# MLP stage: second layer ahead of the transposes, and two low-half subtractions moved from VectorE to GpSimd

## The chip, the cores and the metric

The kernel runs on one core of a Trainium2 chip. The metric is the device time of one execution in microseconds (us). The engines of the core run their own instruction queues and wait for each other through semaphores: TensorE (PE, with its weight loads PEld), VectorE (DVE), ScalarE (ACT), GpSimd (POOL), and SyncE (SP), which here only issues transfers.

## What is computed

The input x has 4 sequences of 1024 tokens of 256 float32 values. A mixture-of-experts feed-forward, an attention block with its own MLP, and the feed-forward again are added to x in turn:

```python
def _ln(x, s, b):
    mu = jnp.mean(x, axis=-1, keepdims=True)
    var = jnp.mean(jnp.square(x - mu), axis=-1, keepdims=True)
    return (x - mu) * jax.lax.rsqrt(var + EPS) * s + b
...
    att = jnp.einsum('bhqk,bhkd->bhqd', p, v).transpose(0, 2, 1, 3).reshape(Bq, Sq, AHD)
    h = att @ Wo + bo + x
    y = _ln(h, lnm_s, lnm_b)
    m = jax.nn.gelu(y @ W1 + b1) @ W2 + b2
    return m + h
...
    x = x + 0.5 * _L0_ffn_ref(_layernorm(x, axis=-1), ...)
    x = x + _L0_attn_ref(_layernorm(x, axis=-1), ...)
    x = x + 0.5 * _L0_ffn_ref(_layernorm(x, axis=-1), ...)
    return x
```

The change lies in the second line of this: att @ Wo with its residual (h), the layer norm of h, and the two-layer MLP (256 to 512 to 256, tanh form of gelu) with its residual.

## The kernel before

The program runs four stages one behind the other: the first feed-forward (names f_), attention (a_), the MLP stage (m_, function mlp_phase), the second feed-forward (g_). Attention leaves its output in HBM as att, transposed; the first feed-forward has left x1 and its layer norm z there. The MLP stage writes x2.

Every float32 matmul is made of three in the type fp32r: each operand is split into a high half (the value rounded to that type, made by ScalarE) and a low half (the value minus the high half), and high x high, high x low and low x high are summed. So each operand costs one ScalarE pass and one subtraction.

The MLP stage goes over the 4096 tokens in 8 blocks of 512 (NB = 8, BT = 512, NT = 4 tiles of 128 rows). For block i:

- SP loads att in two halves (att_in, 1 MB each, L1361), z (zin, 0.5 MB, L1393) and x1 (xin, 0.5 MB, L1405), and stores res (L1401).
- att_hi (ScalarE, L1418) and att_lo (VectorE, L1510) split each half of att, 128 x 2048 elements, into att_s. att_in has one buffer for each half; att_s, zin and xin have two.
- proj (TensorE, L1593): 96 matmuls, in two halves of 48.
- h = proj + zin (VectorE, L1545); statistics (L1548, L1553); rs = (var + eps) ^ -0.5 (GpSimd, L1495, L1497); hn = (h - mean) * rs, four operations of 128 x 256 (VectorE, L1564).
- 8 transposes of hn into PSUM (hT_ps, TensorE, L1623), split by hT_hi (ScalarE, L1440) and hT_lo (VectorE, L1575).
- hid (TensorE, L1649): first layer, 24 matmuls; gelu (ScalarE, L1424); hid_hi (ScalarE, L1432) and hid_lo (VectorE, L1515), four of each.
- acc (TensorE, L1634): second layer, 48 matmuls.
- GpSimd adds bias rows to zin and xin, four operations each (L1478), and adds h to xin (x_h, L1500). res = acc + xin (VectorE, L1584).

The order of the work is written out by hand. Each engine has a function body(i, par), called for i = 0, for pairs of steps in a loop, and for the last ones; in body i the blocks are staggered: the projection is that of block i+1, acc and res are those of block i-1, att_hi and att_lo those of block i+2. An engine issues in program order and stops at each wait. TensorE's body before is: first half of proj(i+1), transposes(i), acc(i-1), second half of proj(i+1), hid(i). SP's body issues z(i+1) behind h(i); then the att loads of block i+3, each behind the att_lo of its half of block i+2; then the store of res(i-1); and last the load of x1(i+1), behind the bias adds of block i, with no way round what stands ahead.

The helper stand_alone(eng, turns) puts an increment of a semaphore that nobody waits for ahead of an instruction.

Of the kernel before, what the change touches and what calls it, by code (L numbers as in the profile page):

```python
# [20 lines left out]
F32 = mybir.dt.float32  # L21
F32R = mybir.dt.float32r
U32 = mybir.dt.uint32
ALU = mybir.AluOpType
# [3 lines left out]
P = 128  # L28
# [7 lines left out]
DC = D // P  # L36
BT = 512
NT = BT // P
# [7 lines left out]
def stand_alone(eng, turns):  # L46


    eng.sem_inc(turns, 1)
# [1238 lines left out]
def mlp_phase(nc, turns, tag, w, att, z, x1, x2):  # L1288
# [9 lines left out]
    with ExitStack() as ctx:  # L1298
# [39 lines left out]
        def over_steps(eng, body):  # L1338

            body(0, 0)  # L1340
            with eng.Fori(0, (NB - 4) // 2) as it:
                body(it * 2 + 1, 1)
                body(it * 2 + 2, 0)
            for i in range(NB - 3, NB + 1):
                body(i, i % 2)

        def has(i, ahead=0):

            return not isinstance(i, int) or 0 <= i + ahead < NB
# [120 lines left out]
        @block.gpsimd  # L1470
        def _(pool):
            pool.memset(mhalf[:], -0.5).then_inc(s["mhalf"], 1)
            pool.wait_ge(s["mhalf"], 1)
            pool.wait_ge(s["w_in"], 16 * NW)

            def add_rows(x, row):
                for t in range(NT):
                    o = pool.tensor_tensor(x[:, t], x[:, t], row[:], ALU.add)  # L1478
                return o

            def z_bias(i, par):
                pool.wait_ge(s["z_in"], i * 16 + 16)
                add_rows(zin[:, par], bo).then_inc(s["zb"], 1)

            def x_bias(i, par):
                pool.wait_ge(s["x_in"], i * 16 + 16)
                add_rows(xin[:, par], b2).then_inc(s["x_b"], 1)
            z_bias(0, 0)

            def body(i, par):  # L1490
                if has(i):
                    x_bias(i, par)
                    pool.wait_ge(s["stats"], i + 1)
                    stand_alone(pool, turns)
                    pool.tensor_scalar(rs[:], mv[:, :, 1], EPS, None, ALU.add).then_inc(s["veps"], 1)  # L1495
                    pool.wait_ge(s["veps"], i + 1)
                    pool.tensor_tensor(rs[:], rs[:], mhalf[:], ALU.pow).then_inc(s["rstd"], 1)  # L1497

                    pool.wait_ge(s["x_b"], i + 1)
                    pool.tensor_tensor(xin[:, par], xin[:, par], h[:], ALU.add).then_inc(s["x_h"], 1)  # L1500
                if has(i, 1):
                    z_bias(i + 1, 1 - par)
            over_steps(pool, body)

        @block.vector
        def _(dve):
# [6 lines left out]
            def hid_lo(i, hc):  # L1513
                dve.wait_ge(s["hid_hi"], i * HC + hc + 1)
                dve.tensor_tensor(hid_s[:, hc, 1], act_out[:, hc], hid_s[:, hc, 0].bitcast(F32),  # L1515
                                  ALU.subtract).then_inc(s["hid_lo"], 1)
# [21 lines left out]
            def body(i, par):  # L1538
                if has(i):
                    dve.wait_ge(s["proj"], i + 1)  # L1540
                    dve.wait_ge(s["zb"], i + 1)
                    if has(i, -1):

                        dve.wait_ge(s["x_h"], i)
                    dve.tensor_tensor(h[:], proj[:], zin[:, par], ALU.add).then_inc(s["h"], 1)  # L1545
                    dve.wait_ge(s["h"], i + 1)
                    for t in range(NT):
                        o = dve.bn_stats(st6[:, t], h[:, t])  # L1548
                    o.then_inc(s["bn"], 1)
                    dve.wait_ge(s["bn"], i + 1)  # L1550
                    stand_alone(dve, turns)
                    for t in range(NT):
                        o = dve.bn_aggr(mv[:, t], st6[:, t])  # L1553
                    o.then_inc(s["stats"], 1)
                if has(i, -1):
                    hid_lo(i - 1, 0)
                    hid_lo(i - 1, 1)
                if has(i):
                    dve.wait_ge(s["rstd"], i + 1)
                    if has(i, -1):  # L1560

                        dve.wait_ge(s["hT_ps"], i * DC)
                    for t in range(NT):
                        o = dve.tensor_scalar(hn[:, t], h[:, t], mv[:, t, 0:1], rs[:, t:t + 1],  # L1564
                                              ALU.subtract, ALU.mult)
                    o.then_inc(s["hn"], 1)
                if has(i, -1):
                    hid_lo(i - 1, 2)
                    hid_lo(i - 1, 3)
                if has(i, 2):  # L1570
                    att_lo(i + 2, par, 0)
                if has(i):
                    for c in range(DC):
                        dve.wait_ge(s["hT_hi"], i * DC + c + 1)
                        dve.tensor_tensor(hT[:, c, 1], hT_ps[:, c], hT[:, c, 0].bitcast(F32),  # L1575
                                          ALU.subtract).then_inc(s["hT_lo"], 1)
                if has(i, 2):
                    att_lo(i + 2, par, 1)
                if has(i, -1):
                    dve.wait_ge(s["acc"], i)  # L1580
                    dve.wait_ge(s["x_h"], i)

                    dve.wait_ge(s["res_out"], i * 16)
                    dve.tensor_tensor(res[:], acc[:], xin[:, 1 - par], ALU.add).then_inc(s["res"], 1)  # L1584
# [3 lines left out]
        def _(pe):  # L1588
# [21 lines left out]
            def body(i, par):  # L1610
                if has(i, 1):
# [1 line left out]

                    pe.wait_ge(s["h"], i + 1)
                    project(i + 1, 1 - par, (0, 1))
                if has(i):
                    pe.wait_ge(s["hn"], i + 1)
                    if has(i, -1):

                        pe.wait_ge(s["hT_lo"], i * DC)  # L1620
                    for c in range(DC):
                        for t in range(NT):
                            o = pe.transpose(hT_ps[:, c, t * P:(t + 1) * P], hn[:, t, c * P:(c + 1) * P], ident[:])  # L1623
                        o.then_inc(s["hT_ps"], 1)
                if has(i, -1):

                    pe.wait_ge(s["hid_lo"], i * HC)
                    if not has(i):

                        pe.wait_ge(s["res"], i - 1)  # L1630
                    for t in range(NT):
                        for hc in range(HC):
                            for a, b in PARTS:
                                o = pe.matmul(acc[:, t], hid_s[:, hc, a, t * P:(t + 1) * P], w2[:, b, hc],  # L1634
                                              start=(t % 2 == 0 and hc == 0 and (a, b) == (0, 0)),
                                              stop=(hc == HC - 1 and (a, b) == PARTS[-1]), skip_group_check=True)
                    o.then_inc(s["acc"], 1)
                if has(i, 1):
                    project(i + 1, 1 - par, (2, 3)).then_inc(s["proj"], 1)
                if has(i):  # L1640
# [81 lines left out]
```

## Time and profile before

| What | Value |
|---|---|
| time of the profiled execution | 2578.13 us |
| its span | 2575.9 us |
| median of 3 runs (lowest, highest) | 2577.75 us (2575.99, 2578.18) |
| MLP stage, first proj matmul to last acc matmul | 2064.8 to 2284.8 us |
| PE busy in the span | 2443.0 us (95%) |
| DVE | 1910.3 us (74%) |
| ACT | 1674.7 us (65%) |
| POOL | 1499.4 us (58%) |

The busy shares say little about the MLP stage, which is 8.5% of the span and in which DVE (142 of 220 us) and POOL (87 of 220) have other shares than in the whole. The timeline of single engines within the stage shows more: a row is a run of equal instructions, with its start, its length, and in brackets how long the engine had been idle before it and which instruction ended that. An idle bracket on TensorE is time lost in this stage if TensorE has work ready behind it.

### The profile page before, as it was taken

Reading aid. Unit: us, or ns where it says so; the run is one execution under the profiler, and the core shown is the slowest. Engines: PE = TensorE matmul, PEld = TensorE weight load, DVE = VectorE, ACT = ScalarE, POOL = GpSimd, SP = SyncE. Lnnn points to the kernel's source line nnn. Section 1 sums busy time; section 2 is a strip of 40 time slices with the busy share of each in tenths; the row PEclk is TensorE's granted clock in tenths of the full one; section 3 lists DMA queues with packets and bytes.
Section 4 is the critical chain, followed back from the end, with each engine's and each line's share of the span. In section 5 each row is a group of like instructions: output and inputs, shape, how many; then the busy total and the mean of one; then the engine's idle time right before and its main releaser. Section 6 shows DMA issues by size and latency. Waiting matters only on the chain. (4 is left out here: it accounts for less than half of the span.)

```text
span 2575.9 us, 46634 instructions
## 1 busy us (share of the span) xinstructions
PE 2443.0 (95%) x14544; PEld 2110.3 (82%) x14544; DVE 1910.3 (74%) x3637; ACT 1674.7 (65%) x2887; POOL 1499.4 (58%) x1519
## 2 busy tenths in 40 slices
PE   6999779999999999999999999999999689959999
PEld 5888768888888888888888888888888488948888
DVE  6777457878878788787887878878778566646665
ACT  3555357878778787787877877778778534233333
POOL 2333167777777777778767777677776244322221
PEclk9999799999999999999999999999999899979999
DMA  4222432213212132122321222212221253321111
GB/s 161 84 96 90 165 116 65 91 49 99 92 43 86 58 95 93 41 82 67 88 90 41 82 81 74 90 41 91 77 70 50 102 174 123 99 88 34 49 49 41
DMA packets 133706, 212.85 MB, mean 83 GB/s; under 512 B 12564, under 2 KB 95816, under 8 KB 125000
## 3 DMA queue, kind: packets, MB, share of 16 engines
q1 hardware_dynamic: 133576, 211.48, 25.5%
q8 instruction: 37, 0.61, 0.1%
q14 instruction: 93, 0.76, 0.1%
HBM read 112.88 MB, written 48.25 MB: 63 GB/s over the span
## 5 line engine op out<-in xcount | busy, mean ns | idle before, releaser
L1168 DVE TENSOR_REDUCE a_nmax<-a_sc 128x1 f32<-128x1024 f32 x512 | 626.6, 1224 | 263.3 <-PE a_sc L1238 253.9
L1099 POOL TENSOR_SCALAR a_pr<-a_pr,a_rden 128x1024 f32<-128x1024 f32 x512 | 575.9, 1126 | 287.7 <-DVE a_rden L1173 226.8
L1029 ACT ACTIVATE a_pT<-a_tr 128x512 fp32r<-128x512 f32 x1024 | 559.6, 596 | 242.1 <-PE a_tr L1250 233.0
L1179 DVE TENSOR_TENSOR a_pT<-a_tr,a_pT 128x512 fp32r<-128x512 f32 x1024 | 650.2, 677 | 18.3 <-ACT a_pT L1029 18.3
L1271 PE MATMUL a_ov<-a_pT,a_v_s 128*128 128x512 f32 x2048 | 604.9, 417 | 1.3 <-DVE a_half L1159 1.3
L1035 ACT ACTIVATE a_pr<-a_sc,a_nmax 128x1024 f32<-128x1024 f32 x512 | 573.7, 1120 | 18.8 <-DVE a_nmax L1168 15.5
L1238 PE MATMUL a_sc<-a_k_s,a_q_s 128*128 128x512 f32 x2048 | 559.7, 395 | 0.4 <-POOL a_v_b L1065 0.4
L1250 PEld LDWEIGHTS a_tr<-a_ident,a_pr 128*128 128x128 f32 x4096 | 475.0, 140 | 96.3 <-DVE a_pT L1179 16.7
L1250 PE MATMUL a_tr<-a_ident,a_pr 128*128 128x128 f32 x4096 | 537.3, 273 | 12.3 <-POOL a_pr L1099 6.2
L1238 PEld LDWEIGHTS a_sc<-a_k_s,a_q_s 128*128 128x128 f32 x2048 | 380.8, 188 | 86.3 <-issue 0.5
L1271 PEld LDWEIGHTS a_ov<-a_pT,a_v_s 128*128 128x128 f32 x2048 | 346.7, 189 | 54.2 <-issue 3.4
L1199 PE MATMUL a_pj<-a_z_s,a_wqk_s 128*128 128x512 f32 x756 | 197.2, 396 | 16.0 <-DMA a_z_s<-zT 15.1
L1199 PEld LDWEIGHTS a_pj<-a_z_s,a_wqk_s 128*128 128x128 f32 x756 | 142.7, 189 | 50.2 <-issue 16.8
L338 ACT ACTIVATE g_act_out<-g_hid,g_b 128x512 f32<-128x512 f32 x72 | 49.6, 689 | 154.9 <-PE g_hid L677 154.9
L1001 ACT ACTIVATE a_staged<-a_pj,a_bqk_s 128x512 f32<-128x512 f32 x126 | 87.1, 691 | 77.1 <-PE a_pj L1199 77.1
L338 ACT ACTIVATE f_act_out<-f_hid,f_b 128x512 f32<-128x512 f32 x72 | 49.3, 684 | 113.8 <-PE f_hid L677 113.8
L709 PEld LDWEIGHTS f_acc<-f_w2p,f_hp 128*128 128x128 f32 x864 | 113.2, 191 | 11.1 <-DVE f_hp L524 5.8
L709 PE MATMUL f_acc<-f_w2p,f_hp 128*128 128x256 f32 x864 | 116.6, 285 | 3.9 <-DVE f_hp L524 3.4
L677 PE MATMUL g_hid<-g_xT,g_w1p 128*128 128x512 f32 x432 | 118.0, 410 | 1.2 <-DVE g_w1p L569 1.2
L677 PE MATMUL f_hid<-f_xT,f_w1p 128*128 128x512 f32 x432 | 117.6, 409 | 1.2 <-DVE f_w1p L569 1.2
L709 PEld LDWEIGHTS g_acc<-g_w2p,g_hp 128*128 128x128 f32 x864 | 111.9, 189 | 7.7 <-DVE g_hp L524 2.1
L709 PE MATMUL g_acc<-g_w2p,g_hp 128*128 128x256 f32 x864 | 115.0, 282 | 0.7 <-DVE g_hp L524 0.5
(220 smaller groups left out, 3219.4 us busy)
## 6 DMA issues: line engine op xcount, KB each, us to landing
a_z_s<-zT SPq DMA_DIRECT2D x32, 1024.0 KB, 7.0
a_k_s<-a_k_s SPq DMA_DIRECT2D x64, 512.0 KB, 5.7
a_wqk_s<-w_split SPq DMA_DIRECT2D x64, 256.0 KB, 3.0
a_v_s<-a_v_b SPq DMA_DIRECT2D x16, 1024.0 KB, 4.6
att<-a_ao SPq DMA_DIRECT2D x32, 512.0 KB, 2.9
m_att_in<-att SPq DMA_DIRECT2D x16, 1024.0 KB, 5.4
a_wv_s<-w_split SPq DMA_DIRECT2D x17, 512.0 KB, 3.8
zT<-f_zT SPq DMA_DIRECT2D x8, 1024.0 KB, 3.9
```

The lines of the kernel that those rows point to most:

```text
L338: act.activation(act_out[:, e % 3], hid[:, (par + e) % 2], ACT.Gelu, bias=b1[:, weights_of(e):weights_of(e) + 1]).then_inc(s["gelu"], 1)
L677: o = pe.matmul(hid[:, (par + e) % 2], w1p[:, a, (c * NE + x) * HID:(c * NE + x + 1) * HID], xT[:, par, c, b], start=(n == 0), stop=(n == 5))
L709: o = pe.matmul(acc[:, t], hp[:, e % 3, a, t * P:(t + 1) * P], w2p[:, b, x * D:(x + 1) * D], start=False, stop=(e == NE - 1 and (a, b) == ...
L1029: act.activation(pT[:, (u // 4) % 2, 0, 4 * part:4 * part + 4, (u % 4) * P:(u % 4 + 1) * P], tr[:, part].rearrange("p (t q) -> p t q", t=4 ...
L1035: act.activation(pr[:, k % NP], sc[:, k % 2], ACT.Exp, bias=nmax[:, k % NP:k % NP + 1], accum_out=den[:, k % NP:k % NP + 1]).then_inc(s["e ...
L1099: pool.tensor_scalar(pr[:, k % NP], pr[:, k % NP], rden[:, k % NP:k % NP + 1], 1.0, ALU.mult, ALU.mult).then_inc(s["normed"], 1)
L1168: dve.tensor_reduce(nmax[:, k % NP:k % NP + 1], sc[:, k % 2], AX.X, ALU.max, negate=True).then_inc(s["negmax"], 1)
L1179: dve.tensor_tensor(to[:, 1], tr[:, part].rearrange("p (t q) -> p t q", t=4), to[:, 0].bitcast(F32), ALU.subtract).then_inc(s["tr_lo"], 1)
L1199: o = pe.matmul(bank[:], wqk_s[:, "QK".index(kind), c, a], z_s[:, c * 2 + b, part], start=(i == 0), stop=(i == 5))
L1238: o = pe.matmul(sc[:, k % 2, kb * BT:(kb + 1) * BT], q_s[:, slot, head, tile * P:(tile + 1) * P], k_s[:, slot, head, a, kb * BT:(kb + 1) * ...
L1250: o = pe.transpose(tr[:, part, j * P:(j + 1) * P], pr[:, (k - LAG) % NP, (4 * part + j) * P:(4 * part + j + 1) * P], ident[:])
L1271: o = pe.matmul(ov[:], v_s[:, vslot, kt, 2 * vhead:2 * vhead + 2] .rearrange("p k f -> p (k f)"), pT[:, blk % 2, a, kt], start=(kt == 0 an ...
```

## The change

In TensorE's body acc(i-1) goes ahead of transposes(i). In VectorE's body the four hid_lo stand together ahead of hn, and the att_lo of blocks 2 to 7 are gone; those of blocks 0 and 1, ahead of the loop, stay on VectorE. GpSimd's body gets them: half 0 behind the residual sum x_h, half 1 behind the bias adds of zin. They wait for att_hi of the same half and for the count of att_lo so far.

```diff
@@ -1487,6 +1487,15 @@
                 add_rows(xin[:, par], b2).then_inc(s["x_b"], 1)
             z_bias(0, 0)
 
+            def att_lo(i, par, half):
+                pool.wait_ge(s["att_hi"], i * 2 + half + 1)
+
+                pool.wait_ge(s["att_lo"], i * 2 + half)
+                stand_alone(pool, turns)
+                g = slice(half * HP, (half + 1) * HP)
+                pool.tensor_tensor(att_s[:, par, 1, g], att_in[:, half], att_s[:, par, 0, g].bitcast(F32),
+                                   ALU.subtract).then_inc(s["att_lo"], 1)
+
             def body(i, par):
                 if has(i):
                     x_bias(i, par)
@@ -1498,8 +1507,12 @@
 
                     pool.wait_ge(s["x_b"], i + 1)
                     pool.tensor_tensor(xin[:, par], xin[:, par], h[:], ALU.add).then_inc(s["x_h"], 1)
+                if has(i, 2):
+                    att_lo(i + 2, par, 0)
                 if has(i, 1):
                     z_bias(i + 1, 1 - par)
+                if has(i, 2):
+                    att_lo(i + 2, par, 1)
             over_steps(pool, body)
 
         @block.vector
@@ -1553,8 +1566,8 @@
                         o = dve.bn_aggr(mv[:, t], st6[:, t])
                     o.then_inc(s["stats"], 1)
                 if has(i, -1):
-                    hid_lo(i - 1, 0)
-                    hid_lo(i - 1, 1)
+                    for hc in range(HC):
+                        hid_lo(i - 1, hc)
                 if has(i):
                     dve.wait_ge(s["rstd"], i + 1)
                     if has(i, -1):
@@ -1564,18 +1577,11 @@
                         o = dve.tensor_scalar(hn[:, t], h[:, t], mv[:, t, 0:1], rs[:, t:t + 1],
                                               ALU.subtract, ALU.mult)
                     o.then_inc(s["hn"], 1)
-                if has(i, -1):
-                    hid_lo(i - 1, 2)
-                    hid_lo(i - 1, 3)
-                if has(i, 2):
-                    att_lo(i + 2, par, 0)
                 if has(i):
                     for c in range(DC):
                         dve.wait_ge(s["hT_hi"], i * DC + c + 1)
                         dve.tensor_tensor(hT[:, c, 1], hT_ps[:, c], hT[:, c, 0].bitcast(F32),
                                           ALU.subtract).then_inc(s["hT_lo"], 1)
-                if has(i, 2):
-                    att_lo(i + 2, par, 1)
                 if has(i, -1):
                     dve.wait_ge(s["acc"], i)
                     dve.wait_ge(s["x_h"], i)
@@ -1613,15 +1619,6 @@
 
                     pe.wait_ge(s["h"], i + 1)
                     project(i + 1, 1 - par, (0, 1))
-                if has(i):
-                    pe.wait_ge(s["hn"], i + 1)
-                    if has(i, -1):
-
-                        pe.wait_ge(s["hT_lo"], i * DC)
-                    for c in range(DC):
-                        for t in range(NT):
-                            o = pe.transpose(hT_ps[:, c, t * P:(t + 1) * P], hn[:, t, c * P:(c + 1) * P], ident[:])
-                        o.then_inc(s["hT_ps"], 1)
                 if has(i, -1):
 
                     pe.wait_ge(s["hid_lo"], i * HC)
@@ -1635,6 +1632,15 @@
                                               start=(t % 2 == 0 and hc == 0 and (a, b) == (0, 0)),
                                               stop=(hc == HC - 1 and (a, b) == PARTS[-1]), skip_group_check=True)
                     o.then_inc(s["acc"], 1)
+                if has(i):
+                    pe.wait_ge(s["hn"], i + 1)
+                    if has(i, -1):
+
+                        pe.wait_ge(s["hT_lo"], i * DC)
+                    for c in range(DC):
+                        for t in range(NT):
+                            o = pe.transpose(hT_ps[:, c, t * P:(t + 1) * P], hn[:, t, c * P:(c + 1) * P], ident[:])
+                        o.then_inc(s["hT_ps"], 1)
                 if has(i, 1):
                     project(i + 1, 1 - par, (2, 3)).then_inc(s["proj"], 1)
                 if has(i):
```

TensorE, one body of the loop. m_proj are the projection halves, m_hT_ps the transposes, m_acc the second layer, m_hid the first. Before:

```order
L1593 MATMUL m_proj<-m_wo,m_att_s 128x256 x48
L1623 MATMUL m_hT_ps<-m_ident,m_hn 128x128 x8
L1627 REGISTER_ALU
L1634 MATMUL m_acc<-m_w,m_hid_s 128x256 x48
L1593 MATMUL m_proj<-m_wo,m_att_s 128x256 x48
L1645 REGISTER_ALU
L1649 MATMUL m_hid<-m_hT,m_w 128x512 x12
```

and after:

```order
L1599 MATMUL m_proj<-m_wo,m_att_s 128x256 x48
L1624 REGISTER_ALU
L1631 MATMUL m_acc<-m_w,m_hid_s 128x256 x48
L1642 MATMUL m_hT_ps<-m_ident,m_hn 128x128 x8
L1599 MATMUL m_proj<-m_wo,m_att_s 128x256 x48
L1651 REGISTER_ALU
L1655 MATMUL m_hid<-m_hT,m_w 128x512 x12
```

The 48 acc matmuls have moved from behind the 8 transposes to ahead of them.

GpSimd, one body of the loop (bias adds of x1, rs, the residual sum into m_xin, bias adds of z). Before:

```order
L1478 TENSOR_TENSOR m_xin<-m_xin,m_b 128x256 x4
L1493 REGISTER_ALU
L1495 TENSOR_SCALAR m_rs<-m_mv 128x4
L1497 TENSOR_TENSOR m_rs<-m_rs,m_mhalf 128x4
L1500 TENSOR_TENSOR m_xin<-m_xin,m_h 128x1024
L1482 ISA
L1478 TENSOR_TENSOR m_zin<-m_zin,m_bo 128x256 x4
```

and after:

```order
L1478 TENSOR_TENSOR m_xin<-m_xin,m_b 128x256 x4
L1504 TENSOR_SCALAR m_rs<-m_mv 128x4
L1506 TENSOR_TENSOR m_rs<-m_rs,m_mhalf 128x4
L1509 TENSOR_TENSOR m_xin<-m_xin,m_h 128x1024
L1491 ISA
L1496 TENSOR_TENSOR m_att_s<-m_att_in,m_att_s 128x2048
L1482 ISA
L1478 TENSOR_TENSOR m_zin<-m_zin,m_bo 128x256 x4
L1491 REGISTER_ALU
L1496 TENSOR_TENSOR m_att_s<-m_att_in,m_att_s 128x2048
```

One subtraction of 128 x 2048 stands directly behind the residual sum, one behind the bias adds of z. ISA and REGISTER_ALU rows are semaphore and register work. SP's and ScalarE's instructions stand in the same order as before; their waits on att_lo are now fulfilled by GpSimd.

## Rows read from the trace of the kernel before

**Rows 1.** Timeline, TensorE in the MLP stage: start us, us, engine, line, operation, out<-in [idle before <-releaser]

```profile
2094.85 5.75 PE L1649 MATMUL m_hid<-m_hT,m_w 128*128 128x512 f32 x24
...
2162.78 1.96 PE L1623 MATMUL m_hT_ps<-m_ident,m_hn 128*128 128x128 f32 x8 [2.76 <-DVE m_hn L1564]
2164.43 7.93 PE L1634 MATMUL m_acc<-m_w,m_hid_s 128*128 128x256 f32 x48
...
2177.90 5.76 PE L1649 MATMUL m_hid<-m_hT,m_w 128*128 128x512 f32 x24
2183.50 5.86 PE L1593 MATMUL m_proj<-m_wo,m_att_s 128*128 128x256 f32 x48
2189.19 1.04 PE L1623 MATMUL m_hT_ps<-m_ident,m_hn 128*128 128x128 f32 x8
2190.26 5.94 PE L1634 MATMUL m_acc<-m_w,m_hid_s 128*128 128x256 f32 x48
...
2201.74 5.76 PE L1649 MATMUL m_hid<-m_hT,m_w 128*128 128x512 f32 x24
...
2251.08 5.75 PE L1649 MATMUL m_hid<-m_hT,m_w 128*128 128x512 f32 x24
...
2268.96 5.76 PE L1649 MATMUL m_hid<-m_hT,m_w 128*128 128x512 f32 x24
2277.34 7.47 PE L1634 MATMUL m_acc<-m_w,m_hid_s 128*128 128x256 f32 x48 [2.62 <-DVE m_hid_s L1515]
```

**Rows 2.** Stretches A:B us: length, busy us of each engine, granted clock, DMA share

```profile
2150.00:2175.00 25.00, 22.24 (x147) 21.12 (x146) 16.82 (x22) 9.63 (x12) 9.82 (x11) 0.86 0.34 112
2175.00:2200.00 25.00, 24.97 (x188) 23.64 (x187) 17.19 (x22) 9.53 (x12) 9.82 (x11) 1.00 0.43 136
```

**Rows 3.** Timeline, GpSimd in the MLP stage

```profile
2082.43 1.04 POOL L1497 TENSOR_TENSOR m_rs<-m_rs,m_mhalf 128x4 f32<-128x4 f32 x1
...
2101.01 2.84 POOL L1478 TENSOR_TENSOR m_xin<-m_xin,m_b 128x256 f32<-128x256 f32 x4 [12.25 <-DMA m_xin<-x]
...
2153.32 3.31 POOL L1478 TENSOR_TENSOR m_xin<-m_xin,m_b 128x256 f32<-128x256 f32 x4 [17.45 <-DMA m_xin<-x]
...
2156.91 1.04 POOL L1497 TENSOR_TENSOR m_rs<-m_rs,m_mhalf 128x4 f32<-128x4 f32 x1
...
2160.26 2.97 POOL L1478 TENSOR_TENSOR m_zin<-m_zin,m_bo 128x256 f32<-128x256 f32 x4
2178.94 2.84 POOL L1478 TENSOR_TENSOR m_xin<-m_xin,m_b 128x256 f32<-128x256 f32 x4 [15.71 <-DMA m_xin<-x]
```

**Rows 4.** Timeline, DMA issues on SP's queue

```profile
2094.74 0.51 SPq L1405 DMA_DIRECT2D m_xin<-x  x1
...
2145.04 1.11 SPq L1405 DMA_DIRECT2D m_xin<-x  x1
...
2174.38 0.46 SPq L1405 DMA_DIRECT2D m_xin<-x  x1
```

**Rows 5.** Timeline, ScalarE: the high half of the attention output

```profile
2165.27 1.90 ACT L1418 ACTIVATE m_att_s<-m_att_in 128x2048 fp32r<-128x2048 f32 x1
...
2190.88 1.92 ACT L1418 ACTIVATE m_att_s<-m_att_in 128x2048 fp32r<-128x2048 f32 x1
```

**Rows 6.** Groups by form, GpSimd and VectorE: out<-in, xcount | busy us, mean ns | idle before

```profile
L1126 POOL TENSOR_TENSOR a_ao<-a_ao,a_half 128x1024 f32<-128x1024 f32 x32 | 76.7, 2395 | 10.6 <-ACT a_ao L1022 10.6
L1065 POOL TENSOR_TENSOR a_v_b<-a_staged,a_v_b 128x256 fp32r<-128x256 f32 x64 | 46.9, 733 | 0.0
...
L1179 DVE TENSOR_TENSOR a_pT<-a_tr,a_pT 128x512 fp32r<-128x512 f32 x1024 | 650.2, 677 | 18.3 <-ACT a_pT L1029 18.3
```

**Rows 7.** Timeline of narrow stretches, GpSimd and VectorE: single hn beside GpSimd

```profile
2130.10 2.79 POOL L1500 TENSOR_TENSOR m_xin<-m_xin,m_h 128x1024 f32<-128x1024 f32 x1
...
2130.54 2.50 DVE L1564 TENSOR_SCALAR m_hn<-m_h,m_mv,m_rs 128x256 f32<-128x256 f32 x1
...
2132.96 0.83 DVE L1564 TENSOR_SCALAR m_hn<-m_h,m_mv,m_rs 128x256 f32<-128x256 f32 x1
```

## Prediction

> **What bounds the kernel now.** I read first the TensorE rows of the MLP stage [rows 1]. The reader is to see three things there. T_i below is the start of the first-layer matmuls of block i-1 (hid, L1649), which is the moment the projection of block i ends: T_1 = 2094.85, T_4 = 2177.90, T_5 = 2201.74, T_7 = 2251.08, T_8 = 2268.96. First, an undisturbed step: from T_4 to T_5 the pieces hid, half a projection, transposes, acc, half a projection follow without a gap, 5.6 + 5.7 + 1.07 + 5.8 + 5.7 = 23.84 us. No step can be shorter than this, and the change removes no TensorE work. Second, the six steps from T_1 to T_7 take 156.23 us, 26.04 each, so 13.2 us in all is stall and what follows a stall. Third, the stall is in one place: the transposes wait 2.76 us for hn at 2162.78, and behind that acc takes 7.93 us where it took 5.94 undisturbed, so a stall costs some 2 us more than its length. Over the 25 us with that stall the granted clock was 0.86 of full speed, in the next 25 it was 1.00 [rows 2]: part of that stretch ran at 1.2 GHz, the lower of the two levels.
>
> Then the GpSimd and queue rows, to see why hn is late [rows 3, 4]. The block of x1 is asked for by SP at 2145.04 and GpSimd's row adds begin at 2153.32, 8.28 us later; the adds take 3.31, the two operations for 1/sqrt end at 2157.95, and only then can hn start. So the stage is set by TensorE in its good steps and by the chain "x load, row adds, rs, hn, transposes" in its bad ones. SP issues that x load after it has waited for the att_lo of both halves and for res. The question for the change is what becomes of that chain.
>
> **TensorE: acc ahead of the transposes.** Nothing is added. The good side: the transposes are now due at T + 5.6 + 5.7 + 5.8 = T + 17.1 where they were due at T + 11.3, so hn has 5.8 us more. The acc matmuls need the four hid_lo at T + 11.3; the last step shows that they are there 8.4 us after T when nothing is in their way (acc at 2277.34 against T_8 = 2268.96) [rows 1], and that is still in time with hid_lo 2 and 3 ahead of hn on VectorE. The other side: whatever hangs on the transposes comes 5.8 us later in the step. That is hT_hi, and behind it on ScalarE att_hi of the second half, which ends 3.61 us after a prompt transpose start (2190.88 + 1.92 against 2189.19) and 4.39 us after a slow one (2165.27 + 1.90 against 2162.78) [rows 1, 5]. The first layer's own wait for hT_lo stays covered by the 5.7 us of the second projection half.
>
> **VectorE: two att_lo fewer.** It loses 2 x 2.3 us a step, none of it on a path that ends last in the trace, because they stand behind hn. Worth nothing by itself. What it has left with an input in PSUM (h, hT_lo, res) isn't held by GpSimd: the a_pT operation, PSUM and SBUF in, takes 677 ns on average over 1024 of them while GpSimd is busy most of the time [rows 6].
>
> **GpSimd: two subtractions more.** The trace has no GpSimd tensor_tensor of 2048 elements. It has 2395 ns for 1024 elements and 733 ns for 256 (this one with the same output type) [rows 6]; the slope is 1662 / 768 = 2.16 ns an element, so 2395 + 1024 x 2.16 = 4.6 us. The bounds are 2 x 2.40 = 4.8 above (the start cost paid twice) and 2048 x 2.16 = 4.4 below (no start cost); I take 4.6. GpSimd's step is then 2.85 + 1.4 + 2.4 + 4.6 + 3.0 + 4.6 = 18.9 us of 23.8: it isn't full, but it is now in two chains. The Trainium skill, page "GPSIMD Engine Reference", section 3.1, gives 4497 ns for a tensor_tensor add of 2048 float32 elements and advises VectorE for such work; by its figure the sum below would be 1 us shorter.
>
> *First chain: hn.* An hn that meets a GpSimd operation is held until that operation ends. The first hn at 2130.54 takes 2.50 us, through the whole of the residual sum x_h that runs from 2130.10 to 2132.89; each hn behind it takes 0.83, one GpSimd row add of 0.75 apart [rows 3, 7]. So the pattern is one hn for each GpSimd operation. With att_lo as GpSimd's next operation behind x_h, the first hn ends with x_h (2.4 + 0.15 after rs), the second with att_lo (4.6 later), the third and fourth one z row add apart each (0.75 + 0.75): hn is complete 8.7 us after rs, where it was 4.6 to 4.7. That no row shows a hold of 4.6 us leaves the second of these open. The Trainium skill, page "SBUF — State Buffer", section "SBUF: two separate sides", says of the port pair shared by VectorE and GpSimd that whoever starts first has it for the whole instruction; by that the hold is 4.6 us as I take it, and if 2.4 us, the longest hold in the rows, were a ceiling, the loop below would be 2.2 us shorter and the sum 11.
>
> *Second chain: SP.* SP waits for att_lo of half 1 (block i+2) before it issues the att load of that half, then the res store, then the x load of block i+1. Those two transfers and the x load now stand behind a GpSimd operation that can't begin before att_hi of half 1. This closes a loop through five engines. From the end e of that att_lo:
> - SP issues att, res, x: two issues ahead of x at 0.5 each (their rows last 0.46 to 0.51) and the start: 1.1 [rows 4].
> - x load to GpSimd's first row add: the rows give 4.56 (2174.38 to 2178.94), 6.27 (2094.74 to 2101.01, an att load issued 0.5 ahead) and 8.28 (2145.04 to 2153.32) [rows 3, 4]. The case is that of 6.27 with a res store of half an att load's size in between too. I take the middle of 6.27 and 8.28, 7.3; ends 4.56 and 8.28.
> - x row adds 2.85, rs 1.4 [rows 3].
> - hn 8.7 (above), its signal 0.1.
> - transposes to the end of att_hi: 3.6 to 4.4, I take 4.0.
> - att_lo on GpSimd: 0.1 + 4.6.
>
> Sum: 1.1 + 7.3 + 2.85 + 1.4 + 8.7 + 0.1 + 4.0 + 0.1 + 4.6 = 30.15 us a step, against 26.04 now and 23.84 for TensorE. TensorE with a slow stretch of 2 to 3 us in each step would need 26 to 27, so it waits and the loop sets the step.
>
> **The sum.** Block 0: rs ends at 2083.47 as before [rows 3]; hn 2092.2, transposes 2092.3, first e = 2092.3 + 4.0 + 0.1 + 4.6 = 2101.0. The loop runs until block 5 (att_lo of block 7 is the last): e of block 4 = 2101.0 + 4 x 30.15 = 2221.6. The transposes of block 5 stand 1.1 + 7.3 + 2.85 + 1.4 + 8.7 + 0.1 = 21.45 later, at 2243.0. Then 1.04 + 5.7 to T_6, and one undisturbed step, because block 6 has no att_lo and no att load on its way: T_7 = 2243.0 + 6.74 + 23.84 = 2273.6, against 2251.08: **+22.5**. Half clock behind the last stall: between 0 and 2, I take **+1**.
>
> The tail loses cover. In block 7 there is no projection. Before, the transposes stood first there and acc hid the way to hT_lo, so hid of block 7 began at T_7 + 17.9 (2268.96 - 2251.08). Now: res of block 5 ends some 1.9 before T_7 and the x load goes out 0.6 later; with 4.56 it is there at T_7 + 3.3, its rows are added at 6.1, rs is there at 7.5, and x_h runs until 9.9. The last hid_lo, ready at 7.6, is held by it: acc at T_7 + 10.2, transposes at 16.0, 1 more for the clock behind the wait for acc, and then 4.0 - 1.9 (att_hi) + 0.7 (the last hT_lo, by the row of the same shape [rows 6]) = 2.8: hid at T_7 + 19.8. That is 1.9 later, **+2**; ends +0.4 (hid_lo not held, prompt clock) and +4. Everything behind it is as before.
>
> The profiled execution took 2578.13 us (its span 2575.9, with 2.2 around it), 0.4 above the median of the runs. 2578.1 + 22.5 + 1 + 2 = **2604**. The small terms' ends: x load at 4.56 throughout -13.5, at 8.28 +5, all transposes slow +2, clock and tail +3: 2590 to 2614.
>
> **Rivals.** *(a) The hn are held by x_h only.* If the semaphore work ahead of att_lo leaves a gap in which VectorE gets all four hn through, hn takes 2.4 + 1.1 = 3.5 and GpSimd's own order is the loop: 1.1 + 7.3 + 2.85 + 1.4 + 2.4 + 4.6 + 3.0 + 4.6 = 27.25. First e = 2083.5 + 2.4 + 4.6 + 3.0 + 4.6 = 2098.0, block 4 at 2207.0, transposes of block 5 at 2223.2, T_7 at 2253.7, with the tail 2578.1 + 2.6 + 2 = 2583. For it: the operation ahead carries waits that a row add doesn't. Against: each row add took its turn with hn one for one.
>
> *(b) The other side, faster.* TensorE sets the step, from the point where the loop is under about 24.5 us. Place: the x load of each step. If it comes back in 4.56 as at 2174.38 and hn is free as in (a), the loop is 24.5, block 4's e = 2196.2, transposes of block 5 = 2209.7, T_7 = 2240.3, 10.8 under before, and with the tail 2578.1 - 10.8 + 2 = 2569. Against: an att load now goes out just ahead of every x load, which the 4.56 row didn't have within 4 us.
>
> *(c) The clock.* If stalls of 3 to 5 us in each step keep the lower clock for more than the next stretch, TensorE's 23.84 us grow towards twice that and TensorE is the bound again: with half of each step at it, 36 us a step, 2640. Against: behind 2.76 us of waiting only one stretch was slow.
>
> *(d) The change doesn't do what it says.* The order excerpts show the operations where the diff puts them, so no chance is given to this.
>
> **How the numbers follow.** Forecast 0.74 (2590 to 2614, value 2604), (a) 0.14, (b) 0.07, (c) 0.05. A measurement of this kernel tells about 0.2%, 5 us, from no change. (a) at 2583 lies at that edge, with its x term spreading it to both sides: I give most of it to "same". Faster 0.08, same 0.11, slower 0.81. The range 2579 to 2614 holds the forecast and most of (a) and leaves out (b) and (c).
>
> **What would show it.** Right: T_i to T_i+1 of 29 to 31 us in the five steps up to T_6, the last ones near 24 and 18 to 21; the transposes waiting for hn 3 to 5 us in each of them; one hn of 4.6 us or more in each block with an att_lo behind x_h; GpSimd's m_att_s rows at 4.5 to 4.8 us; the x load issued about 1 us behind the second of them; att_lo of half 1 waiting for ScalarE. Wrong: hn as a whole under 5 us (then (a)); TensorE without waits at the transposes (then (b)); acc or the projection at double length through whole steps (then (c)).

## Result: slower by 1.1%, and where the time went

| What | before | after |
|---|---|---|
| median of 4 runs | 2577.97 us | 2607.38 us |
| lowest, highest | 2575.99, 2578.70 us | 2602.61, 2608.75 us |
| ratio to before, 95% interval | 1 | 1.0112 [1.0095, 1.013] |
| span of the profiled execution | 2575.9 us | 2604.3 us |

2604 us was predicted, range 2579 to 2614. From the page of after, the busy times and the granted clock in its 40 slices of 65 us. In the last line, the 8 8 9 of the closing 7 8 8 9 7 9 9 9 9 lie wholly within the MLP stage; the page of before has 9 9 9 there:

```profile
PE 2448.9 (94%) x14544; PEld 2116.3 (81%) x14544; DVE 1904.0 (73%) x3625; ACT 1675.2 (64%) x2887; POOL 1552.5 (60%) x1531
...
PEclk9999799999999999999999999999999788979999
```

The timeline of TensorE in the MLP stage of after (start us, us, engine, line, operation [idle before <-releaser]) answers to [rows 1]. L1655 is hid, L1642 the transposes, L1631 acc, L1599 the projection:

```profile
2090.40 1.97 PE L1642 MATMUL m_hT_ps<-m_ident,m_hn 128*128 128x128 f32 x8 [5.96 <-DVE m_hn L1577]
...
2119.88 1.97 PE L1642 MATMUL m_hT_ps<-m_ident,m_hn 128*128 128x128 f32 x8 [3.90 <-DVE m_hn L1577]
...
2151.06 1.97 PE L1642 MATMUL m_hT_ps<-m_ident,m_hn 128*128 128x128 f32 x8 [5.06 <-DVE m_hn L1577]
2152.68 7.34 PE L1599 MATMUL m_proj<-m_wo,m_att_s 128*128 128x256 f32 x48
2159.86 5.76 PE L1655 MATMUL m_hid<-m_hT,m_w 128*128 128x512 f32 x24
...
2182.29 1.96 PE L1642 MATMUL m_hT_ps<-m_ident,m_hn 128*128 128x128 f32 x8 [5.30 <-DVE m_hn L1577]
...
2213.43 1.97 PE L1642 MATMUL m_hT_ps<-m_ident,m_hn 128*128 128x128 f32 x8 [5.39 <-DVE m_hn L1577]
...
2244.66 1.97 PE L1642 MATMUL m_hT_ps<-m_ident,m_hn 128*128 128x128 f32 x8 [5.72 <-DVE m_hn L1577]
...
2252.80 5.76 PE L1655 MATMUL m_hid<-m_hT,m_w 128*128 128x512 f32 x24
...
2276.34 5.76 PE L1655 MATMUL m_hid<-m_hT,m_w 128*128 128x512 f32 x24
2286.47 8.56 PE L1631 MATMUL m_acc<-m_w,m_hid_s 128*128 128x256 f32 x48 [4.37 <-DVE m_hid_s L1528]
...
2297.48 5.87 PE L1655 MATMUL m_hid<-m_hT,m_w 128*128 128x512 f32 x24 [1.57 <-DVE m_hT L1583]
```

A stretch of 30 us of after (busy us of each engine, granted clock, DMA share, GB/s), which answers to [rows 2]:

```profile
2140.00:2170.00 30.00, 24.94 (x170) 23.64 (x170) 16.58 (x20) 9.63 (x12) 17.25 (x12) 0.89 0.39 122
```

The transposes now wait for hn in every block up to 5: 5.96 us in block 0, 3.90 in block 1 and 5.1 to 5.7 in blocks 2 to 5 (31.3 us over six waits). From block 1 on they stand 31.18, 31.23, 31.14 and 31.23 us apart, where TensorE's own work is 23.84. Behind each wait one stretch is slow (transposes 1.97 for 1.04, half a projection 6.7 to 7.5 for 5.85), and the granted clock over such stretches is 0.89 of full speed, so part of them ran at 1.2 GHz, against 1.00 in an undisturbed one of before [rows 2]. T_6 to T_7 is 2252.80 to 2276.34, 23.54 us: block 6 has no att_lo and no wait.

One turn of the loop, in the timelines of GpSimd, SP and ScalarE of after, which answer to [rows 3, 4, 5]. GpSimd:

```profile
2124.47 4.57 POOL L1496 TENSOR_TENSOR m_att_s<-m_att_in,m_att_s 128x2048 fp32r<-128x2048 f32 x1 [3.47 <-ACT m_att_s L1418]
2138.37 2.82 POOL L1478 TENSOR_TENSOR m_xin<-m_xin,m_b 128x256 f32<-128x256 f32 x4 [9.32 <-DMA m_xin<-x]
2141.15 0.23 POOL L1504 TENSOR_SCALAR m_rs<-m_mv 128x4 f32<-128x4 f32 x1
2141.46 1.04 POOL L1506 TENSOR_TENSOR m_rs<-m_rs,m_mhalf 128x4 f32<-128x4 f32 x1
...
2155.67 4.58 POOL L1496 TENSOR_TENSOR m_att_s<-m_att_in,m_att_s 128x2048 fp32r<-128x2048 f32 x1 [3.39 <-ACT m_att_s L1418]
```

SP's queue in the same turn:

```profile
2129.85 0.41 SPq L1401 DMA_DIRECT2D x<-m_res  x1
2130.35 0.46 SPq L1405 DMA_DIRECT2D m_xin<-x  x1
```

ScalarE, att_hi of half 1:

```profile
2153.56 1.90 ACT L1418 ACTIVATE m_att_s<-m_att_in 128x2048 fp32r<-128x2048 f32 x1
```

Read in the order of time, the turn from the end of one att_lo of half 1 (2124.47 + 4.57 = 2129.04) to the next (2155.67 + 4.58 = 2160.25):

| Piece | predicted | measured | from |
|---|---|---|---|
| att_lo ends, SP issues att, res, x | 1.1 | 1.31 | 2130.35 |
| x load until GpSimd adds | 7.3 | 8.02 | 2138.37 |
| bias adds of x1 | 2.85 | 2.78 | 2141.15 |
| rs | 1.4 | 1.35 | 2142.50 |
| four hn, start of the transposes | 8.8 | 8.56 | 2151.06 |
| transposes, hT_hi, att_hi | 4.0 | 4.40 | 2153.56 + 1.90 |
| att_lo on GpSimd with its start | 4.7 | 4.79 | 2160.25 |
| sum | 30.15 | 31.21 | |

The x load takes its 8.0 us while all 16 DMA engines are busy, as the stretch from its issue to its arrival shows (DMA share 1.00, 334 GB/s):

```profile
2131.00:2138.00 7.00, 7.00 (x46) 6.32 (x45) 3.79 (x11) 5.90 (x9) 0.00 (x0) 1.00 1.00 334
```

In flight together there are the att load of 1 MB (issued at 2129.23), the res store and the x load of 0.5 MB each, and the z load of the next block, 0.5 MB, which SP issues 0.64 us behind x and which the prediction did not count.

GpSimd's idle brackets tell the same from its side: it waits 9.3 us for the x load and 3.4 us for ScalarE's att_hi in each turn, so it is never full; it is busy some 18.5 us of 31.2. The hn one by one, beside GpSimd, in narrow timelines that answer to [rows 7]:

```profile
2142.63 2.38 DVE L1577 TENSOR_SCALAR m_hn<-m_h,m_mv,m_rs 128x256 f32<-128x256 f32 x1 [5.43 <-POOL m_rs L1506]
2144.93 4.60 DVE L1577 TENSOR_SCALAR m_hn<-m_h,m_mv,m_rs 128x256 f32<-128x256 f32 x1
2149.46 0.81 DVE L1577 TENSOR_SCALAR m_hn<-m_h,m_mv,m_rs 128x256 f32<-128x256 f32 x1
```

GpSimd beside it:

```profile
2142.47 2.39 POOL L1509 TENSOR_TENSOR m_xin<-m_xin,m_h 128x1024 f32<-128x1024 f32 x1
2144.82 4.57 POOL L1496 TENSOR_TENSOR m_att_s<-m_att_in,m_att_s 128x2048 fp32r<-128x2048 f32 x1
```

The second hn takes 4.60 us: it began 0.11 us behind the start of GpSimd's att_lo and ended 0.14 behind its end.

### The profile page after: what moved, and what is told of

Its sections match the earlier page's. It is cut to its first block and busy times, and to the rows that moved or that the text cites. A ratio compares the mean times of both kernels' runs of the same rounds, so it can differ in the third digit from the quotient of the medians.

```text
span 2604.3 us, 46646 instructions
## 1 busy us (share of the span) xinstructions
PE 2448.9 (94%) x14544; PEld 2116.3 (81%) x14544; DVE 1904.0 (73%) x3625; ACT 1675.2 (64%) x2887; POOL 1552.5 (60%) x1531
## 5 line engine op out<-in xcount | busy, mean ns | idle before, releaser
L1250 PE MATMUL a_tr<-a_ident,a_pr 128*128 128x128 f32 x4096 | 537.2, 273 | 12.6 <-DVE a_pT L1179 6.3
```

What stands on the lines that cost most here:

```text
L1250: o = pe.transpose(tr[:, part, j * P:(j + 1) * P], pr[:, (k - LAG) % NP, (4 * part + j) * P:(4 * part + j + 1) * P], ident[:])
```

## Experiments

All are timed against the kernel before on the same chip. The two theories in the expectations are the loop (GpSimd's subtraction of half 1, SP's queue, the x load, hn, the transposes, att_hi) and, as the main rival, one of its parts by itself. In the diffs "-" is the changed kernel or, where it says so, the kernel before.

### Order only

GpSimd's att_lo of both halves are taken out of the changed kernel (the first lines), and VectorE has them again (the others). "..." marks lines left out:

```diff
-                if has(i, 2):
-                    att_lo(i + 2, par, 0)
                 if has(i, 1):
                     z_bias(i + 1, 1 - par)
-                if has(i, 2):
-                    att_lo(i + 2, par, 1)
...
+                if has(i, 2):
+                    att_lo(i + 2, par, 0)
                 if has(i):
                     for c in range(DC):
                         dve.wait_ge(s["hT_hi"], i * DC + c + 1)
...
+                if has(i, 2):
+                    att_lo(i + 2, par, 1)
```

> The order of acc and transposes (and the four hid_lo together) as in the changed kernel, but every att_lo stays on VectorE: half 0 behind hn, half 1 behind hT_lo. Theory (the slowdown is a loop through the x load that GpSimd's two subtractions close): without them hn ends 4.7 us behind rs and not 8.5, and att_lo of half 1 ends some 6.7 us behind the start of the transposes and not 9.2, so the loop has about 24.5 us, next to TensorE's 23.84. Steps of 23.9 to 24.6 us, about 2570 us, faster than the kernel before. Rival (the transposes put late are what costs, since everything behind them moves by 5.8 us): steps stay near 30 us, 2600 us or more.

Measured: 2566.91 us (before 2577.81), ratio 0.9964 [0.995, 0.9979]. The transposes (L1633) in this kernel's timeline:

```profile
2133.38 1.09 PE L1633 MATMUL m_hT_ps<-m_ident,m_hn 128*128 128x128 f32 x8 [0.15 <-DVE m_hn L1564]
...
2157.62 1.09 PE L1633 MATMUL m_hT_ps<-m_ident,m_hn 128*128 128x128 f32 x8 [0.47 <-DVE m_hn L1564]
...
2181.82 1.09 PE L1633 MATMUL m_hT_ps<-m_ident,m_hn 128*128 128x128 f32 x8 [0.44 <-DVE m_hn L1564]
...
2205.97 1.09 PE L1633 MATMUL m_hT_ps<-m_ident,m_hn 128*128 128x128 f32 x8 [0.41 <-DVE m_hn L1564]
```

The same stretch of 30 us in this kernel:

```profile
2140.00:2170.00 30.00, 29.52 (x204) 27.13 (x203) 21.80 (x34) 12.63 (x17) 9.39 (x11) 1.00 0.56 182
```

The transposes wait 0.15 to 0.47 us and stand 24.2 us apart. They have the place behind acc that the change gives them, 17.3 to 17.6 us behind T. So the late transposes aren't what costs; alone, that half of the change is a gain of 0.36%, 11 us. From T_1 to T_7 it wins 12.6 us (143.6 for 156.23), and 1.7 are lost again in the tail (hid of block 7 begins 19.6 us behind T_7, where it was 17.9). It takes away the stalls of the kernel before, and with them the lower clock: granted 1.00 in that stretch and in the four others from 2084 to 2230.

### GpSimd's part only

The kernel before, with both att_lo of blocks 2 to 7 in GpSimd's body as in the change, TensorE and hid_lo untouched ("-" is the kernel before). The first part is GpSimd's body, the second VectorE's; the definition of att_lo on GpSimd, added as in the change, is left out:

```diff
...
+                if has(i, 2):
+                    att_lo(i + 2, par, 0)
                 if has(i, 1):
                     z_bias(i + 1, 1 - par)
+                if has(i, 2):
+                    att_lo(i + 2, par, 1)
...
-                if has(i, 2):
-                    att_lo(i + 2, par, 0)
...
-                if has(i, 2):
-                    att_lo(i + 2, par, 1)
```

> Only GpSimd's part of the change: both att_lo of blocks 2 to 7 on GpSimd, TensorE and hid_lo in the order of the kernel before. Theory (loop): the loop doesn't run through acc, so it keeps its 31.2 us a step; the transposes of block 5 stand near 2245, T_7 near 2282, and the tail is that of the kernel before: 2609 us, 2603 to 2614. Rival (it takes both parts, the late transposes and the late subtraction): 2578 to 2590.

Measured: 2612.77 us, ratio 1.0133 [1.0116, 1.015]. The transposes of blocks 1 to 5 in its timeline:

```profile
2120.63 1.97 PE L1632 MATMUL m_hT_ps<-m_ident,m_hn 128*128 128x128 f32 x8 [8.26 <-DVE m_hn L1577]
...
2152.53 1.97 PE L1632 MATMUL m_hT_ps<-m_ident,m_hn 128*128 128x128 f32 x8 [6.04 <-DVE m_hn L1577]
...
2183.81 1.96 PE L1632 MATMUL m_hT_ps<-m_ident,m_hn 128*128 128x128 f32 x8 [4.45 <-DVE m_hn L1577]
...
2215.44 1.97 PE L1632 MATMUL m_hT_ps<-m_ident,m_hn 128*128 128x128 f32 x8 [5.09 <-DVE m_hn L1577]
...
2247.47 1.97 PE L1632 MATMUL m_hT_ps<-m_ident,m_hn 128*128 128x128 f32 x8 [5.85 <-DVE m_hn L1577]
```

They are 31.9, 31.3, 31.6 and 32.0 us apart. The whole loss comes from GpSimd's half of the change. The intervals of this ratio and of 1.0112 for the whole change overlap, so the runs don't show whether the new order wins anything beside it. The expectation, 2609, was 4 us low, within its range. One cause can be read in the trace: GpSimd's operations ahead of hn meet VectorE's hid_lo here (the bias adds at 2170.09 take 3.35 us for 2.8, the second operation of rs 1.42 for 1.04), which I had not counted.

### The x load out of the loop

SP in the changed kernel stores res and loads x1 ahead of the att load of half 1:

```diff
                 if has(i, 3):
-                    for half in range(2):
-
-                        sp.wait_ge(s["att_lo"], (i + 2) * 2 + half + 1)
-                        load_att(ahead, half)
+                    sp.wait_ge(s["att_lo"], (i + 2) * 2 + 1)
+                    load_att(ahead, 0)
                 if has(i, -1):
                     sp.wait_ge(s["res"], i)
...
                     sp.dma_start(xin[:, 1 - par], x_from).then_inc(s["x_in"], 16)
+                if has(i, 3):
+                    sp.wait_ge(s["att_lo"], (i + 2) * 2 + 2)
+                    load_att(ahead, 1)
```

> The changed kernel, with SP storing res and loading x1 ahead of the att load of half 1, so that neither waits for GpSimd's second subtraction. Theory (loop): x is asked for some 6 us behind the transposes and lands at 11, rs is there at 15.3 and hn at 23.8, next to TensorE's 23.84: steps of 23.9 to 25 us, T_7 about 8 under the kernel before, tail +3: 2574 us, 2568 to 2582. Rival (the hold of hn by GpSimd's subtraction sets the step by itself, whoever waits on SP): steps stay over 29 us, about 2600.

Measured: 2571.83 us, ratio 0.9978 [0.9968, 0.9988]. GpSimd's timeline over a step of this kernel:

```profile
2141.17 4.61 POOL L1497 TENSOR_TENSOR m_att_s<-m_att_in,m_att_s 128x2048 fp32r<-128x2048 f32 x1 [3.34 <-ACT m_att_s L1419]
2146.33 3.29 POOL L1479 TENSOR_TENSOR m_xin<-m_xin,m_b 128x256 f32<-128x256 f32 x4 [0.55 <-DMA m_xin<-x]
...
2151.19 2.78 POOL L1510 TENSOR_TENSOR m_xin<-m_xin,m_h 128x1024 f32<-128x1024 f32 x1
2153.94 5.05 POOL L1497 TENSOR_TENSOR m_att_s<-m_att_in,m_att_s 128x2048 fp32r<-128x2048 f32 x1
2158.95 3.02 POOL L1479 TENSOR_TENSOR m_zin<-m_zin,m_bo 128x256 f32<-128x256 f32 x4
```

GpSimd waits 0.55 us for x where it waited 9.3. Both subtractions are on GpSimd and last as long (4.6 to 5.06), one hn is still held by the first (the four hn take 6.9 us), and yet the transposes stand 24.0 to 24.2 us apart (2113.26, 2137.30, 2161.53, 2185.61, 2209.70). The hold alone doesn't set the step. It costs where the loop is closed, and the place where it is closed is SP's queue.

### The hold, measured by its length

GpSimd's subtraction of half 0 in four pieces of 128 x 512, one behind the other:

```diff
-                g = slice(half * HP, (half + 1) * HP)
-                pool.tensor_tensor(att_s[:, par, 1, g], att_in[:, half], att_s[:, par, 0, g].bitcast(F32),
-                                   ALU.subtract).then_inc(s["att_lo"], 1)
+                n = HP if half == 0 else 1
+                for k in range(n):
+                    w_ = HP // n
+                    g = slice(half * HP + k * w_, half * HP + (k + 1) * w_)
+                    o = pool.tensor_tensor(att_s[:, par, 1, g], att_in[:, half, k * w_:(k + 1) * w_],
+                                           att_s[:, par, 0, g].bitcast(F32), ALU.subtract)
+                o.then_inc(s["att_lo"], 1)
```

> The changed kernel, with GpSimd's subtraction of half 0 in four pieces of 128 x 512 (1.2 to 1.3 us each). Theory (each hn is held until the GpSimd operation it meets ends): hn is x_h 2.4 and three pieces, 6.3 us behind rs and not 8.5, the loop 29.0 and not 31.2: 2594 us. Rival (the two engines share by rate and the length of one operation doesn't matter): hn stays at 8.4 us and the time at 2607; the pieces' start costs of 0.2 each would only add.

Measured: 2591.27 us, ratio 1.005 [1.0033, 1.0067]: 16 us of the loss are gone, though GpSimd has more work than with one piece (5.17 us for 4.57). Three single hn of one block:

```profile
2170.10 1.38 DVE L1581 TENSOR_SCALAR m_hn<-m_h,m_mv,m_rs 128x256 f32<-128x256 f32 x1
2171.40 1.35 DVE L1581 TENSOR_SCALAR m_hn<-m_h,m_mv,m_rs 128x256 f32<-128x256 f32 x1
2172.67 1.35 DVE L1581 TENSOR_SCALAR m_hn<-m_h,m_mv,m_rs 128x256 f32<-128x256 f32 x1
```

and the pieces on GpSimd:

```profile
2169.98 1.34 POOL L1499 TENSOR_TENSOR m_att_s<-m_att_in,m_att_s 128x512 fp32r<-128x512 f32 x1
2171.29 1.31 POOL L1499 TENSOR_TENSOR m_att_s<-m_att_in,m_att_s 128x512 fp32r<-128x512 f32 x1
2172.56 1.31 POOL L1499 TENSOR_TENSOR m_att_s<-m_att_in,m_att_s 128x512 fp32r<-128x512 f32 x1
```

Each hn now ends 0.15 us behind one piece. The four take 6.2 us and not 8.4, and the transposes come every 28.2 to 29.1 us. Sharing by rate would have left hn at 8.4.

### The x load ahead of the store only

```diff
                 if has(i, -1):
                     sp.wait_ge(s["res"], i)
-                    sp.dma_start(to, res[:]).then_inc(s["res_out"], 16)
                 if has(i, 1):

                     sp.wait_ge(s["x_b"], i + 1)
                     sp.dma_start(xin[:, 1 - par], x_from).then_inc(s["x_in"], 16)
+                if has(i, -1):
+                    sp.dma_start(to, res[:]).then_inc(s["res_out"], 16)
```

> The changed kernel, with SP issuing the x load of 0.5 MB ahead of the store of res, still behind the att load of half 1. Theory (loop, the x load's 8.0 us is queueing behind 1.5 MB): the load goes out 0.5 us sooner and comes back some 1.5 us faster, loop 29.2 and not 31.2: 2597 us, 2594 to 2601. Rival (the load's time has nothing to do with what goes out just ahead): 0.5 us a step, 2604.

Measured: 2601.84 us, ratio 1.0089 [1.0073, 1.0104], between the two expectations and just above the range of the first. From its rows: issued at 2131.73, 2160.88, 2190.87 and 2220.69, with the adds at 2138.70, 2168.13, 2197.82 and 2228.00, the load takes 7.0, 7.3, 7.0 and 7.3 us where it took 8.0. The transposes are 29.5 to 30.3 us apart. So 0.5 MB less ahead of the load is worth 0.7 to 1.0 us, with 0.5 more for the earlier issue; I had counted 1.5 and 0.5. The z load right behind x counts for little: in the second experiment it goes out 5 us later (2136.62), and x was used 8.9 us behind the issue of the att load (2130.03 to 2138.95), against 9.1 in the changed kernel (2129.23 to 2138.37). In the changed kernel itself the first turn shows the same: no res exists yet, the load issued at 2100.04 is used at 2106.66, 6.6 us, and that turn has 29.5 us and not 31.2.

### Both subtractions behind the bias adds of z

```diff
-                if has(i, 2):
-                    att_lo(i + 2, par, 0)
                 if has(i, 1):
                     z_bias(i + 1, 1 - par)
                 if has(i, 2):
+                    att_lo(i + 2, par, 0)
+                if has(i, 2):
                     att_lo(i + 2, par, 1)
```

> The changed kernel, with both of GpSimd's subtractions behind the bias adds of z. Theory (loop): hn is held as in the kernel before, 4.7 us, so the way through the transposes is 4 us shorter; then GpSimd's own order is the longest way, rs to the end of the second subtraction 2.4 + 3.0 + 4.6 + 4.6 = 14.6, with 1.3 + 8.0 + 2.85 + 1.35 a loop of 28.1 us: 2589 us. Rival (the hold of hn is the whole loss): TensorE-bound steps of 24 us, about 2571.

Measured: 2587.16 us, ratio 1.0032 [1.0018, 1.0045]. One step of GpSimd:

```profile
2163.45 2.38 POOL L1509 TENSOR_TENSOR m_xin<-m_xin,m_h 128x1024 f32<-128x1024 f32 x1
2165.78 2.96 POOL L1478 TENSOR_TENSOR m_zin<-m_zin,m_bo 128x256 f32<-128x256 f32 x4
2168.72 4.63 POOL L1496 TENSOR_TENSOR m_att_s<-m_att_in,m_att_s 128x2048 fp32r<-128x2048 f32 x1
2173.52 4.61 POOL L1496 TENSOR_TENSOR m_att_s<-m_att_in,m_att_s 128x2048 fp32r<-128x2048 f32 x1 [0.17 <-POOL m_att_s L1496]
```

VectorE in the same step, the four hn:

```profile
2163.60 4.56 DVE L1577 TENSOR_SCALAR m_hn<-m_h,m_mv,m_rs 128x256 f32<-128x256 f32 x4 [6.94 <-POOL m_rs L1506]
```

hn is back at 4.56 us, as in the kernel before, and the transposes come every 27.9 to 28.5 us. GpSimd has no gap but 0.17 us between rs and the end of the second subtraction: its own order is the way through the loop now, as the 28.1 us of the expectation had it. So of the 7.4 us between 31.2 and 23.84, taking the hold away wins 3.1, until the next way round is the longest; the rest stays as long as SP's x load stands behind GpSimd.

### The last body, and the three together

Order only, with the old order kept in body 7 (transposes ahead of acc, hn ahead of hid_lo 2 and 3), and the same with SP's order as in the third experiment. TensorE's part of it, with turn() for the transposes and second() for acc:

```diff
...
+                if isinstance(i, int) and i == NB - 1:
+                    turn()
+                    second()
+                else:
+                    second()
+                    turn()
```

> As x1_order_only, but in body 7, where no projection is left, the transposes stay ahead of acc and hn ahead of hid_lo 2 and 3, as in the kernel before. Theory (in that body acc was the cover of the way from the transposes to hT_lo, and acc ahead waits for a hid_lo that x_h holds): the hid matmuls of block 7 begin 18 us behind T_7 and not 19.6: 2564 to 2566 us. Rival (the last body is bound by something else, the x load): no difference, 2567.

> As x7_order_and_tail, and SP stores res and loads x1 ahead of the att load of half 1. Theory: the four steps of 24.2 us, where the transposes wait 0.4 us for hn, become TensorE's 23.84, 1.5 us in all: 2563 us. Rival (the x load is no more in any chain that ends last): the same as x7_order_and_tail.

Measured: 2569.12 us, ratio 0.9963 [0.9949, 0.9977], and 2565.08 us, ratio 0.9947 [0.9934, 0.9961]. Both are faster than the kernel before by about 0.4 to 0.5%; the intervals of the two, and that of order only, overlap, so the runs don't tell the three apart. The first came out above both of its expectations (2564 to 2566, and 2567 for the rival), the second 2 us above its own. In the profiles, the old order in body 7 gained nothing: hid of block 7 begins 19.5 us behind T_7 (2237.23 to 2256.71) against 19.6 with the order only (2236.18 to 2255.79). The wait moved from acc to the transposes, as TensorE's timeline has it:

```profile
2237.23 5.75 PE L1658 MATMUL m_hid<-m_hT,m_w 128*128 128x512 f32 x24
2247.97 1.97 PE L1639 MATMUL m_hT_ps<-m_ident,m_hn 128*128 128x128 f32 x8 [4.99 <-DVE m_hn L1565]
...
2256.71 5.76 PE L1658 MATMUL m_hid<-m_hT,m_w 128*128 128x512 f32 x24
```

They wait 4.99 us for hn, whose x arrives at T_7 + 2.4 because res of block 5, and behind it the x load, stand behind the transposes of body 6. That was my rival for it. In the profile of the second, taking the x load out of the loop did what was expected, though its time doesn't show it beyond noise: no transposes but the first and the last wait for hn, and they stand 23.6 us apart (2112.50, 2136.09, 2159.68, 2183.22, 2206.82). That is TensorE's own step in the new order, 0.25 less than the 23.84 that the prediction called the shortest possible, read from the old order.

## Why the prediction was right, point by point

- **The bound of the kernel before.** Right: with the stalls before the transposes gone (order only), the stage runs at 24.2 us a step, next to TensorE's own, and wins 12.6 us up to T_7 of the 13.2 that were given for stalls; the tail takes 1.7 of them back.
- **A loop through five engines replaces it.** Right, and it is what the sum rested on. Two experiments cut it at different places (no GpSimd subtraction; x load ahead of the wait), and either cut brings the step from 31.2 to between 24.0 and 24.2 us.
- **Rival (a), hn held by x_h only.** Wrong: hn takes 8.35 to 8.45 us in blocks 0 to 5. The semaphore work ahead of the subtraction left no gap that VectorE could use; the second hn began 0.11 us behind it.
- **The hold lasts the whole 4.6 us.** Right, by the row of 4.60 us and by the four pieces. The Trainium skill, page "SBUF — State Buffer", section "SBUF: two separate sides", gives the port pair that the two engines share to the one that starts first, for the whole instruction. This case's trace agrees: att_lo began 0.11 us ahead, and the hn took 4.60 us beside its 4.57.
- **GpSimd's price.** 4.54 to 4.62 us were measured for the 4.6 expected. The 4497 ns that the prediction sets beside its own term are 0.1 us short of it.
- **The x load.** The term that was mis-sized: 7.3 taken, 8.0 to 8.1 measured, each turn but the first. Together with 0.4 for the transposes to att_hi, always on the slow side of my two ends, it makes 31.2 of 30.15. Over four turns that would be 4.2 us; the first turn had no res store and took 29.4 from the end of one att_lo to the next, which leaves 2.5. The way from the last of these att_lo to the transposes of block 5 took 22.0 us for 21.45, and the start and the end of the way 0.3 more than worked out. Together it is 3.3: from the end of rs of block 0 to T_7 194.5 us (2081.88 to 2276.34) against 191.1 predicted.
- **The tail.** +2 predicted, +3.3 measured: 21.1 us from T_7 to hid of block 7, where it was 17.9. acc began 10.1 behind T_7, where 10.2 was worked out, but that agreement is partly luck. x was there at T_7 + 2.0 and not 3.3, and x_h ended at 8.9 and not 9.9. It held the third hid_lo and not the last one (2.44 us, from 2283.38), and the fourth then followed from 2285.74 to 2286.42. What was missed is that acc took 8.56 us, 2.6 over an undisturbed one, where I had 1.
- **The sum.** Counted from the end of rs of block 0, T_7 is 26.9 us later than before, where 22.5 + 1 was predicted. But rs of block 0 itself ended 1.6 us earlier (2081.88 against 2083.47), ahead of anything that the change touches; in the second experiment it ended at 2083.50. 26.9 + 3.3 - 1.6 = 28.6, and the spans differ by 28.4. Predicted were 25.5. So the loop and the tail came out 4.6 us above the prediction, mainly by the x load, att_hi and the clock behind the last wait, and a start that was early by chance gave 1.6 of them back.
- **Rival (b)**, faster, wasn't this kernel. The third experiment gets to its side by another way than the one named: with the x load ahead of one wait in SP's queue, and with an hn still held, the step is 24.0 to 24.2 us with the same GpSimd work. **Rival (c)**, the clock, was wrong: one slow stretch behind each wait and no more.

## What to carry to other kernels

Before work is moved to an idle engine, ask who waits for its end and what is queued behind that wait: here SP's queue with its fixed order made the x load of the next step wait behind an att load of a later one, which waited for its buffer, and the idle engine became a link of a loop though it was never full. Sum such a loop once round and compare it with the step of the bound engine; that, and not the busy share, tells what a moved operation costs. And a change of two parts should be timed as two: one part here was worth -0.4%, the other +1.3%, and both together +1.1%.

## What the runs showed of the hardware

- A GpSimd tensor_tensor on SBUF holds a VectorE tensor_scalar on SBUF for its whole length: 4.60 us for one of 4.57, and 1.35 to 1.38 us each for pieces of 1.31 to 1.34. In these rows the two take turns, one hn for each GpSimd operation, also where GpSimd's next operation has semaphore waits of its own.
- GpSimd's cost is nearly all slope: 2048 elements in 4.58 us, four times 512 in 5.17 us, 0.2 us for each of the three operations more. The four were measured with an hn beside each.
- A load of 0.5 MB was used 4.6 us after its issue, with a store of 0.5 MB 0.5 us ahead of it and the last load 4 us away (2174.38 to 2178.94 in the kernel before); 6.6 us with a load of 1 MB close ahead; 8.0 with both, issued within 1.3 us; and 7.0 to 7.3 when that store went out behind it. In the last three a z load of 0.5 MB followed 0.6 to 1.7 us behind. The DMA engines were busy 1.00 of the time in the stretch of the 8.0 us, and 0.79 in that of the 4.6 (2175 to 2179).
